# Five ready tiles of attention weights and two exponential slots, in place of four and three, in a two-layer graph kernel

## The chip, the cores and the metric

One core of one Trainium2 chip runs the whole program. The metric is device time in microseconds (us): 262.67 us is the median of three runs of the kernel before, which lie between 262.58 and 264.55. Lower is better.

## The reference

The input is x (2048 nodes, 256 features, float32) and a sparse 0/1 adjacency matrix adj (2048 x 2048). Two graph layers follow each other. Cut to what matters:

```python
h = relu(layernorm(x))
# layer 0: masked attention, a graph convolution, and two sigmoid gates
hd = h @ W_sa
scores = (hd @ a_l)[:, None] + (hd @ a_r)[None, :]
e = where(adj != 0, exp(-leaky_relu(scores, 0.01)), 0.0)
x_a = e / (e.sum(1, keepdims=True) + 1e-05) @ hd
x_b = adj @ (h @ W_gcnb) + b_gcnb
x = x + sigmoid(gate_a * x_a + gate_b * x_b)
# layer 1: attention inside each graph of 64 nodes (ptr), other pairs masked with -1e6
h = relu(layernorm(x))
q, k, v = h @ Wq.T + bq, h @ Wk.T + bk, h @ Wv.T + bv
s = (where(same, q @ k.T / 16, 0) + 2 * adj) * where(same, 1, -1e6)
x = x + (softmax(s) * same) @ v
```

## The kernel before

Five engines run programs written out by hand (one function per engine, under `block.sync`, `block.gpsimd`, `block.scalar`, `block.tensor`, `block.vector`), tied together by semaphores alone. Nothing reorders an engine's program: it issues in the order of the text, and a wait stops all that stands behind it on that engine.

**Layer 0** is a loop over four stages k (columns of 512 nodes each, `CW`), and in a stage over eight pairs q of 128-row tiles. The pair's number over all stages is g = 8k + q. A pair's attention weights (128 x 1024 values) are made in four steps:

- `raw(g)` on ACT (L624, two instructions): the exponential, in float32, into slot g mod `SLOTS` of `e_slot`
- `mask(g)` on DVE (L1462): that slot times the adjacency, in place
- `high(g)` on ACT (L631): the float16 high half of the slot, into place g mod `RING` of `e_hi`
- `low(g)` on DVE (L1468): what the high half left over, into place g mod `RING` of `e_lo`

TensorE (PE) then sums the pair in `attend(k, j)`: for each of its two tiles, 12 matmuls (L972, L974, L976) into the four banks A. Between them it runs `sums(k + 1, ...)`, the graph convolution of the next stage (L948, 16 matmuls a pair). Stage 3 has no such sums.

Three waits bound how far the steps may run ahead. `raw(g)` waits until `low(g - SLOTS)` is done, since it overwrites that slot. `high(g)` waits until PE has attended pair g - `RING`. `attend` waits for `low(g)`.

ACT and DVE run in step with PE by program order: in iteration g of the loop, ACT has `raw(g + RING)` and then `high(g + RING - 1)`, and DVE has `mask(g + RING)` and then `low(g + RING - 1)`. Other work stands between: on DVE `keep_b` (sums into `xb`), `gate_sums`, `add_mix`, `counts` (from L1584 on) and others. At a stage's start (q = 0, k >= 1) DVE first has `denominators(k - 1)` (L1614), which waits until PE has attended the whole stage before; then ACT has `keep_a` (L693, the results out of the banks A) and two tanh. `attend(k, 0)` writes those banks and waits for `keep_a`; in stages 1 and 2 it stands behind 16 `sums`.

Ahead of the loop ("the lead-in"), the first weights are made between the last products of the layer's setup: ACT has `hd_high(g)` (L616, out of PE's banks), `raw(0..3)`, `high(0..2)`, and as its last copy `keep_row(3)` (L608, the row of scores `s_row`). PE's loop starts with `query_key` (L985), and that waits for `keep_row(3)`. DVE has `hd_low`, `mask(0..3)`, `low(0..2)` and the last two `keep_b(0, r)`.

After pair 31 comes **layer 1**, a pipeline over eight pairs p of tiles: PE turns h1 (L1019), ACT and DVE split it into halves (`h1T_high` L723, `h1T_low` L1657), and PE multiplies (`keys`, `values`, L896) and so on. Its first steps stand inside stage 3 already: `turn_h1(0)` in pair 29, `keys(0)` between the two tiles of pair 30. `keys(0)` waits for `h1T_low(0)`, which on DVE stands behind the last `low`, `shifts` and `counts`.

Of the kernel before, what the change touches and what calls it, by code (L numbers as in the profile page):

```python
# [6 lines left out]
F32 = mybir.dt.float32  # L7
# [23 lines left out]
def two_graph_layers(nc, x, adj, adj_t, W_sa, W_saT, a_col, W_gcnb, b_gcnb, gate_w, gate_b, ptr,  # L31
                     Wq, Wk, WvT, bq_bk, bv, out):
    N, D = x.shape
# [3 lines left out]
    KT = D // P  # L37
    CT = 4
    NC = NT // CT
    CW = CT * P  # L40
    RING, SLOTS = 4, 3
    NQ = NT // 2
    PAIRS = NQ * NC
    PW = 2 * CW
# [7 lines left out]
    with ExitStack() as ctx:  # L52
        def sb(name, shape, dt=F32):
            return ctx.enter_context(nc.sbuf_tensor(name, shape, dt))
# [9 lines left out]
        e_slot = sb("e_slot", [P, SLOTS * PW])  # L64
        e_hi = sb("e_hi", [P, RING * PW], F16)
        e_lo = sb("e_lo", [P, RING * PW], F16)
# [113 lines left out]
        w_sa = e_slot[:, 0:KT * D].rearrange("p (k d) -> p k d", k=KT)  # L180
        w_b = e_slot[:, 512:512 + KT * WB].rearrange("p (k d) -> p k d", k=KT)
        w_cols = w_b[:, :, D:WB]
        cols_sq = e_slot[:, 2064:2064 + KT * 6].rearrange("p (k c) -> p k c", k=KT)
        w_saT = e_slot[:, 1040:1040 + KT * D].rearrange("p (k d) -> p k d", k=KT)
        junk_a = e_hi[:, :].bitcast(F32)[:, 0:3 * KT * D].rearrange("p (w k d) -> p w k d", w=3, k=KT)
        at_least = e_lo[:, 0:NT * NP].bitcast(BF16).rearrange("p (t c) -> p t c", c=NP)
# [25 lines left out]
        score_row = adjt[:, 2 * NT * D + N:2 * NT * D + 2 * N]  # L212
        c_all = adjt[:, 3 * NT * D:3 * NT * D + NT]
        mask_row = s_row
        fac_row = e_hi[:, :].bitcast(F32)
        prob_row = e_lo[:, :].bitcast(F32)
        probT_row = e_slot


# [163 lines left out]
        def wait(eng, signal, value):  # L383
            if value > 0:
                eng.wait_ge(signal, value)
# [9 lines left out]
        def adjt_words(k, j, first, count):  # L395
            at = (k % 2) * CHUNK + j * CW + first
            return adjt[:, at:at + count]

        def slot_words(g):
            return e_slot[:, (g % SLOTS) * PW:(g % SLOTS + 1) * PW]  # L400

        def high_words(g):
            return e_hi[:, (g % RING) * PW:(g % RING + 1) * PW]

        def low_words(g):
            return e_lo[:, (g % RING) * PW:(g % RING + 1) * PW]
# [176 lines left out]
        def _(eng):  # L583
# [22 lines left out]
            def keep_row(c):  # L606
                eng.wait_ge(rows_summed, c + 1)
                eng.activation(s_row[:, c * CW:(c + 1) * CW], L[:, (c + 1) % 2, :], ACT.Copy) \  # L608
                   .then_inc(rows_kept, 1)
# [9 lines left out]
            def raw(g):  # L619
                k = g // NQ  # L620
                wait(eng, lo_ready, g - SLOTS + 1)
                for n in range(2):
                    j = 2 * (g % NQ) + n
                    ins = eng.activation(slot_words(g)[:, n * CW:(n + 1) * CW], s_row[:, k * CW:(k + 1) * CW],  # L624
                                         ACT.Exp, scale=SLOPE - 1.0, bias=nbias[:, j:j + 1])
                ins.then_inc(raw_ready, 1)

            def high(g):
                eng.wait_ge(mask_ready, g + 1)
                wait(eng, slot_free, g - RING + 1)  # L630
                eng.activation(high_words(g), slot_words(g), ACT.Copy, scale=E_SCALE).then_inc(hi_ready, 1)  # L631
# [50 lines left out]
            hd_high(7)  # L682
            raw(3)
            high(2)
            keep_row(3)
            eng.wait_ge(rows_kept, NC)
            eng.activation(es[:, :], hc[:, :, 2], ACT.Exp, scale=SLOPE, bias=rm[:, 3:4]).then_inc(es_made, 1)
# [588 lines left out]
        def _(eng):  # L1276
# [174 lines left out]
            def keep_b(k, r):  # L1451
                eng.wait_ge(b_summed, CT * k + r + 1)
                eng.tensor_copy(tails[:, r, :], B[:, r % 2, D:D + TAIL]).then_inc(tail_kept, 1)
                eng.scalar_tensor_tensor(out=xb[:, k % 2, r, :], in0=B[:, r % 2, 0:D], scalar=norm_h[:, 0:1],  # L1454
                                         in1=bg_row[:, :], op0=ALU.mult, op1=ALU.add).then_inc(b_kept, 1)

            def mask(g):
                k, q = divmod(g, NQ)
                if q % 2 == 0:
                    eng.wait_ge(adjt_loaded[q // 2], 16 * (k + 1))  # L1460
                eng.wait_ge(raw_ready, g + 1)
                eng.scalar_tensor_tensor(out=slot_words(g), in0=slot_words(g), scalar=1.0,  # L1462
                                         in1=adjt_words(k, 2 * q, 0, PW), op0=ALU.min, op1=ALU.mult) \
                   .then_inc(mask_ready, 1)

            def low(g):
                eng.wait_ge(hi_ready, g + 1)
                eng.scalar_tensor_tensor(out=low_words(g), in0=slot_words(g), scalar=E_SCALE,  # L1468
                                         in1=high_words(g), op0=ALU.mult, op1=ALU.subtract) \
                   .then_inc(lo_ready, 1)  # L1470
# [19 lines left out]
            hd_low(7)  # L1490
            mask(3)
            low(2)
            keep_b(0, 2)
            keep_b(0, 3)
            eng.wait_ge(layer1_loaded, 16 * 5)
            for kk in range(KT):
# [382 lines left out]
```

## Time and profile before

| what | value |
|---|---|
| median of three runs | 262.67 us |
| the profiled execution | 260.9 us, its span 259.1 us |
| PE busy | 227.5 us, 88% of the span |
| DVE busy | 191.8 us, 74% |
| ACT busy | 158.5 us, 61% |
| granted TensorE clock, mean | 0.991 of full |
| chain that ended last | PE 69%, DVE 15%, ACT 8%, issue 4% of the span |
| `attend` (L972, L974, L976) | 768 matmuls of 128 x 257 |
| `sums` (L948) | 512 matmuls |

A row of the timeline gives an instruction's start, its duration, its engine and line, and in brackets how long its engine stood idle before it and what ended that. Two instructions in a row on ACT or DVE start closer together than the duration that stands beside each, because the next starts before the former has landed. The four stages of the loop run from about 59 to about 208 us; layer 1's steps overlap the last of it.

### The profile page before, as it was taken

How to read it: one execution, taken by the hardware profiler on the slowest of the kernel's cores; microseconds unless marked ns; L12 is line 12 of the kernel's file. 1: busy time of each engine (PE TensorE's matmuls, PEld its weight loads, DVE VectorE, ACT ScalarE, POOL GpSimd, SP SyncE). 2: the span in 40 equal slices, each digit the busy share in tenths (PEclk: the TensorE clock that was granted, in tenths of full speed). 3: DMA queues.
4: the chain of work that ended last, by engine and by line, in shares of the span. 5: the costliest groups of instructions: out<-in, count | busy, mean ns of one | idle time of the engine just before them, and what ended most of it. 6: DMA issues, size and time to landing. Idle time of an engine off the chain costs nothing.

```text
span 259.1 us, 5318 instructions
## 1 busy us (share of the span) xinstructions
PE 227.5 (88%) x2032; PEld 192.9 (74%) x2032; DVE 191.8 (74%) x481; ACT 158.5 (61%) x303; POOL 37.9 (15%) x77
## 2 busy tenths in 40 slices
PE   0688999998998999999999999999967849599962
PEld 0557887887886888888888888878855747488851
DVE  3589878699695686699963999936993366787864
ACT  3568727896666683946736937439865343577650
POOL 2442400000020000011000011000220112434440
PEclk9999999999999999999999999999997999999999
DMA  6999296029874000840400000000000000011113
GB/s 177 343 389 334 27 393 250 3 77 343 277 277 166 0 3 6 320 162 5 160 0 4 1 3 0 3 0 3 0 0 3 0 1 3 1 42 43 62 62 127
DMA packets 20091, 26.34 MB, mean 102 GB/s; under 512 B 1888, under 2 KB 11872, under 8 KB 20064
## 3 DMA queue, kind: packets, MB, share of 16 engines
q1 hardware_dynamic: 19520, 25.72, 28.9%
q8 instruction: 17, 0.28, 0.4%
q10 hardware_dynamic: 544, 0.27, 0.4%
q14 instruction: 10, 0.08, 0.1%
HBM read 23.88 MB, written 2.10 MB: 100 GB/s over the span
## 4 chain that ended last, share of the span: by engine, by line
PE 69%; DVE 15%; ACT 8%; issue 4%; DMA 2%; SPq 1%; DVEq 0%; ACTq 0%
PE bank_b L948 20%; PE bank_a L972 9%; PE bank_a L974 9%; PE bank_a L976 8%; PE bank_a L896 7%; PE bank_l L896 4%; PE bank_b L896 3%; DVE e_lo L1468 2%; DMA e_slot<-in_W_saT 2%; PE bank_a L1087 2%; PE bank_l L888 1%; DVE st6b L1641 1%; ACT adjt L591 1%; PE bank_a L1065 1%; DVE x_all L1636 1%
## 5 line engine op out<-in xcount | busy, mean ns | idle before, releaser
L972 PE MATMUL bank_a<-hd,e_hi 128*128 128x257 f16 x256 | 70.3, 275 | 1.5 <-DVE e_lo L1468 0.9
L974 PE MATMUL bank_a<-hd,e_hi 128*128 128x257 f16 x256 | 70.7, 276 | 0.0
L976 PE MATMUL bank_a<-hd,e_lo 128*128 128x257 f16 x256 | 69.9, 273 | 0.0
L948 PE MATMUL bank_b<-hb,adjt 128*128 128x259 f16 (+1 forms) x512 | 66.7, 273 | 0.2 <-DVE xb L1454 0.2
L948 PEld LDWEIGHTS bank_b<-hb,adjt 128*128 128x128 bf16 x512 | 49.4, 97 | 7.3 <-DVE xb L1454 0.5
L631 ACT ACTIVATE e_hi<-e_slot 128x1024 f16<-128x1024 f32 x32 | 33.7, 1052 | 33.8 <-PE bank_a L976 19.9
L1462 DVE SCALAR_TENSOR_TENSOR e_slot<-e_slot,adjt 128x1024 f32<-128x1024 f32 x32 | 39.0, 1219 | 8.6 <-ACT e_slot L624 8.6
L1468 DVE SCALAR_TENSOR_TENSOR e_lo<-e_slot,e_hi 128x1024 f16<-128x1024 f32 x32 | 39.0, 1220 | 8.5 <-ACT e_hi L631 8.5
L624 ACT ACTIVATE e_slot<-s_row,nbias 128x512 f32<-128x512 f32 x64 | 42.3, 710 | 0.3
L972 PEld LDWEIGHTS bank_a<-hd,e_hi 128*128 128x128 f16 x256 | 25.0, 98 | 6.4 <-DVE e_lo L1468 1.3
L976 PEld LDWEIGHTS bank_a<-hd,e_lo 128*128 128x128 f16 x256 | 25.4, 99 | 3.5
L974 PEld LDWEIGHTS bank_a<-hd,e_hi 128*128 128x128 f16 x256 | 24.9, 97 | 3.5
L542 POOL TENSOR_TENSOR rs_all<-veb,half_neg 128x2 f32<-128x2 f32 x8 | 7.3, 917 | 110.9 <-DVE veb L1646 110.9
L896 PE MATMUL bank_l<-adjt,w_qk 128*128 128x256 f16 x96 | 12.5, 282 | 7.0 <-DVE adjt L1657 7.0
L896 PEld LDWEIGHTS bank_l<-adjt,w_qk 128*128 128x128 f16 x96 | 9.1, 100 | 9.6 <-DVE adjt L1657 5.3
L1664 DVE SCALAR_TENSOR_TENSOR adjt<-bank_l,u_s,adjt 128x256 f16<-128x256 f32 x16 | 7.0, 480 | 11.7 <-ACT adjt L730 11.7
L693 ACT ACTIVATE xa<-bank_a,ga 128x256 f32<-128x256 f32 x16 | 6.3, 474 | 14.2 <-DVE ga L1621 14.2
L547 POOL TENSOR_TENSOR adjt<-adjt 128x512 f16<-128x512 f32 x8 | 9.3, 1156 | 32.5 <-ACT adjt L736 32.5
L896 PE MATMUL bank_a<-wb,x_all 128*128 128x262 f16 x96 | 12.9, 287 | 0.7 <-issue 0.6
L896 PE MATMUL bank_b<-w_v,adjt 128*128 128x257 f16 x96 | 12.7, 273 | 0.0
L896 PE MATMUL bank_a<-wsa,x_all 128*128 128x256 f16 x96 | 11.8, 272 | 0.4 <-DVE hd L1447 0.4
L896 PEld LDWEIGHTS bank_a<-wb,x_all 128*128 128x128 f16 x96 | 9.6, 102 | 3.1 <-issue 1.0
(216 smaller groups left out, 347.9 us busy)
## 6 DMA issues: line engine op xcount, KB each, us to landing
adjt<-in_adj_t SPq DMA_DIRECT2D x16, 1024.0 KB, 7.9
x_all<-in_x SPq DMA_DIRECT2D x4, 512.0 KB, 5.4
out<-adjt SPq DMA_DIRECT2D x16, 128.0 KB, 1.8
adjt<-in_x SPq DMA_DIRECT2D x3, 512.0 KB, 8.1
diag<-in_adj SPq DMA_DIRECT2D x16, 64.0 KB, 3.5
adjt<-in_x SPq DMA_DIRECT2D x2, 256.0 KB, 3.7
e_slot<-in_L_gnn_W_gcnb ACTq DMA_DIRECT2D x1, 256.0 KB, 3.9
e_slot<-in_W_saT SPq DMA_DIRECT2D x1, 256.0 KB, 5.1
```

The source lines that it names most:

```text
L542: eng.tensor_tensor(rs_all[:, first:last], veb[:, r0:r1], half_neg[:, 0:r1 - r0], ALU.pow) \
L547: eng.tensor_tensor(v16[:, p % 4, :, 1, :], v32[:, p % 2, :, :], v16[:, p % 4, :, 0, :], ALU.subtract) \
L624: ins = eng.activation(slot_words(g)[:, n * CW:(n + 1) * CW], s_row[:, k * CW:(k + 1) * CW], ACT.Exp, scale=SLOPE - 1.0, bias=nbias[:, j:j ...
L631: eng.activation(high_words(g), slot_words(g), ACT.Copy, scale=E_SCALE).then_inc(hi_ready, 1)
L896: mm = eng.matmul(bank, left(kk, a), right(kk, b), start=(kk == 0 and a + b == 0), stop=(kk == KT - 1 and a == 1))
L948: eng.matmul(B[:, r % 2, 0:cols], adjt_block(k, j, r), hb16[:, j, part, 0:cols], start=(j == 0 and part == 0), stop=(j == NT - 1 and part ...
L972: eng.matmul(A[:, r, 0:D + 1], high, hd16[:, j, 0, 0:D + 1], start=(j == 0), stop=False, skip_group_check=True)
L974: eng.matmul(A[:, r, 0:D + 1], high, hd16[:, j, 1, 0:D + 1], start=False, stop=False, skip_group_check=True)
L976: mm = eng.matmul(A[:, r, 0:D + 1], low, hd16[:, j, 0, 0:D + 1], start=False, stop=(j == NT - 1), skip_group_check=True)
L1462: eng.scalar_tensor_tensor(out=slot_words(g), in0=slot_words(g), scalar=1.0, in1=adjt_words(k, 2 * q, 0, PW), op0=ALU.min, op1=ALU.mult) \
L1468: eng.scalar_tensor_tensor(out=low_words(g), in0=slot_words(g), scalar=E_SCALE, in1=high_words(g), op0=ALU.mult, op1=ALU.subtract) \
L1664: eng.scalar_tensor_tensor(out=gT16[:, p % 3, c, 1, :], in0=KEYS[:, c * 2 * P:(c + 1) * 2 * P], scalar=u_s[:, c:c + 1], in1=gT16[:, p % 3, ...
```

## The change

The ring of ready weights has five places in place of four, and `e_slot` two slots in place of three. `e_hi` and `e_lo` grow by 2,048 bytes a partition each, and `e_slot` shrinks by 4,096. Two views into the smaller or larger tiles are cut to fit. Since the loop makes `raw(g + RING)` in iteration g, a fifth pair has to be started ahead of it: `raw(4)`, `high(3)`, `mask(4)` and `low(3)` move from the loop's first iteration into the lead-in, and each later step of the loop stands one pair earlier. By the same formula `raw(g)` now waits for `low(g - 2)`.

```diff
-    RING, SLOTS = 4, 3
+    RING, SLOTS = 5, 2
...
-        cols_sq = e_slot[:, 2064:2064 + KT * 6].rearrange("p (k c) -> p k c", k=KT)
+        cols_sq = e_slot[:, 1552:1552 + KT * 6].rearrange("p (k c) -> p k c", k=KT)
...
-        fac_row = e_hi[:, :].bitcast(F32)
-        prob_row = e_lo[:, :].bitcast(F32)
+        fac_row = e_hi[:, 0:2 * N].bitcast(F32)
+        prob_row = e_lo[:, 0:2 * N].bitcast(F32)
...
             raw(3)
             high(2)
+            raw(4)
+            high(3)
             keep_row(3)
...
             low(2)
+            mask(4)
             keep_b(0, 2)
+            low(3)
             keep_b(0, 3)
```

The lead-in on ACT before, from `hd_high(5)` to the first `raw` of the loop (`hd` is written by `hd_high`, `e_slot` by `raw`, `e_hi` by `high`, `s_row` by `keep_row`):

```order
L616 ACTIVATE hd<-bank_a,dp_g 128x256 [waits hd_summed]
L616 ACTIVATE hd<-bank_a,dp_g 128x256
L624 ACTIVATE e_slot<-s_row,nbias 128x512 x2
L616 ACTIVATE hd<-bank_a,dp_g 128x256 [waits hd_summed]
L616 ACTIVATE hd<-bank_a,dp_g 128x256
L631 ACTIVATE e_hi<-e_slot 128x1024 [waits mask_ready]
...
L624 ACTIVATE e_slot<-s_row,nbias 128x512 [waits lo_ready]
L624 ACTIVATE e_slot<-s_row,nbias 128x512
L631 ACTIVATE e_hi<-e_slot 128x1024 [waits mask_ready]
L608 ACTIVATE s_row<-bank_l 128x512 [waits rows_summed]
L687 ACTIVATE es<-hc,rm 128x16 [waits rows_kept]
```

The same place in the changed kernel:

```order
L624 ACTIVATE e_slot<-s_row,nbias 128x512 [waits lo_ready]
L624 ACTIVATE e_slot<-s_row,nbias 128x512
L616 ACTIVATE hd<-bank_a,dp_g 128x256 [waits hd_summed]
...
L624 ACTIVATE e_slot<-s_row,nbias 128x512 [waits lo_ready]
L624 ACTIVATE e_slot<-s_row,nbias 128x512
L631 ACTIVATE e_hi<-e_slot 128x1024 [waits mask_ready]
L624 ACTIVATE e_slot<-s_row,nbias 128x512 [waits lo_ready]
L624 ACTIVATE e_slot<-s_row,nbias 128x512
L631 ACTIVATE e_hi<-e_slot 128x1024 [waits mask_ready]
L608 ACTIVATE s_row<-bank_l 128x512 [waits rows_summed]
L689 ACTIVATE es<-hc,rm 128x16 [waits rows_kept]
```

`raw(2)` has gained a wait on `lo_ready`, and `raw(4)` and `high(3)` now stand ahead of `keep_row(3)`.

Stage 3 on DVE before, from the `mask` of pair 30 to `counts` (`e_slot` is written by `mask`, `e_lo` by `low`, `x_all` to `veb` by `add_mix`, `nb_all` by `shifts`, `owned` by `counts`):

```order
L1462 SCALAR_TENSOR_TENSOR e_slot<-e_slot,adjt 128x1024 [waits raw_ready,adjt_loaded3]
L1468 SCALAR_TENSOR_TENSOR e_lo<-e_slot,e_hi 128x1024 [waits hi_ready]
L1636 SCALAR_TENSOR_TENSOR x_all<-xa,x_all 128x512 [waits half_ready,th_ready]
...
L1646 TENSOR_SCALAR veb<-mvb 128x2 [waits mvb_ready]
L1462 SCALAR_TENSOR_TENSOR e_slot<-e_slot,adjt 128x1024 [waits raw_ready]
L1468 SCALAR_TENSOR_TENSOR e_lo<-e_slot,e_hi 128x1024 [waits hi_ready]
L1651 SCALAR_TENSOR_TENSOR nb_all<-mvb,rs_all 128x2 [waits rs_ready] x2
L1468 SCALAR_TENSOR_TENSOR e_lo<-e_slot,e_hi 128x1024 [waits hi_ready]
L1584 TENSOR_TENSOR owned<-tails,onehot 128x4x34 x2
```

And in the changed kernel, from the `mask` of pair 31:

```order
L1464 SCALAR_TENSOR_TENSOR e_slot<-e_slot,adjt 128x1024 [waits raw_ready]
L1470 SCALAR_TENSOR_TENSOR e_lo<-e_slot,e_hi 128x1024 [waits hi_ready]
L1640 SCALAR_TENSOR_TENSOR x_all<-xa,x_all 128x512 [waits half_ready,th_ready]
...
L1650 TENSOR_SCALAR veb<-mvb 128x2 [waits mvb_ready]
L1470 SCALAR_TENSOR_TENSOR e_lo<-e_slot,e_hi 128x1024 [waits hi_ready]
L1655 SCALAR_TENSOR_TENSOR nb_all<-mvb,rs_all 128x2 [waits rs_ready] x2
L1588 TENSOR_TENSOR owned<-tails,onehot 128x4x34 x2
```

One `mask` and one `low` fewer stand in stage 3; they have moved through the stages ahead of it into the lead-in.

## Rows read from the trace of the kernel before

**Rows 1.** Waits of PE by what ended them: total us, times, longest us

```profile
PE bank_l L896 <- DVE adjt L1657: 7.0, 3, 3.3
...
PE bank_a L972 <- DVE e_lo L1468: 0.9, 1, 0.9
```

**Rows 2.** Timeline of ACT, lead-in: start us, duration us, instruction, [idle before <-releaser]

```profile
51.74 1.33 ACT L624 ACTIVATE e_slot<-s_row,nbias 128x512 f32<-128x512 f32 x2
53.22 0.84 ACT L616 ACTIVATE hd<-bank_a,dp_g 128x256 f16<-128x256 f32 x2
...
56.15 1.33 ACT L624 ACTIVATE e_slot<-s_row,nbias 128x512 f32<-128x512 f32 x2
57.37 1.05 ACT L631 ACTIVATE e_hi<-e_slot 128x1024 f16<-128x1024 f32 x1
58.32 0.59 ACT L608 ACTIVATE s_row<-bank_l 128x512 f32<-128x512 f32 x1
```

**Rows 3.** Timeline of DVE, lead-in

```profile
51.24 1.22 DVE L1468 SCALAR_TENSOR_TENSOR e_lo<-e_slot,e_hi 128x1024 f16<-128x1024 f32 x1
...
54.51 1.22 DVE L1462 SCALAR_TENSOR_TENSOR e_slot<-e_slot,adjt 128x1024 f32<-128x1024 f32 x1
55.65 1.22 DVE L1468 SCALAR_TENSOR_TENSOR e_lo<-e_slot,e_hi 128x1024 f16<-128x1024 f32 x1
```

**Rows 4.** Timeline of PE, the loop's first instruction

```profile
59.17 1.97 PE L985 MATMUL bank_l<-wqk_in 128*128 128x256 f32 x8 [1.02 <-ACT s_row L608]
```

**Rows 5.** Timeline of DVE, stage 1, from its start to stage 2's

```profile
101.41 0.16 DVE L1614 SCALAR_TENSOR_TENSOR den<-es,bank_a 128x4 f32<-128x4 f32 x1 [0.73 <-issue]
...
106.44 1.22 DVE L1462 SCALAR_TENSOR_TENSOR e_slot<-e_slot,adjt 128x1024 f32<-128x1024 f32 x1 [2.06 <-ACT e_slot L624]
...
110.66 1.22 DVE L1468 SCALAR_TENSOR_TENSOR e_lo<-e_slot,e_hi 128x1024 f16<-128x1024 f32 x1
...
116.04 1.23 DVE L1462 SCALAR_TENSOR_TENSOR e_slot<-e_slot,adjt 128x1024 f32<-128x1024 f32 x1
117.18 1.22 DVE L1468 SCALAR_TENSOR_TENSOR e_lo<-e_slot,e_hi 128x1024 f16<-128x1024 f32 x1
...
120.72 1.21 DVE L1462 SCALAR_TENSOR_TENSOR e_slot<-e_slot,adjt 128x1024 f32<-128x1024 f32 x1
121.86 1.22 DVE L1468 SCALAR_TENSOR_TENSOR e_lo<-e_slot,e_hi 128x1024 f16<-128x1024 f32 x1
...
137.13 0.16 DVE L1614 SCALAR_TENSOR_TENSOR den<-es,bank_a 128x4 f32<-128x4 f32 x1 [2.14 <-PE bank_a L976]
```

**Rows 6.** Timeline of ACT, stage 1

```profile
105.01 1.32 ACT L624 ACTIVATE e_slot<-s_row,nbias 128x512 f32<-128x512 f32 x2
...
123.11 1.34 ACT L624 ACTIVATE e_slot<-s_row,nbias 128x512 f32<-128x512 f32 x2
```

**Rows 7.** Timeline of PE, stage 3's first `attend`, then two of layer 1's `keys`

```profile
174.26 0.27 PE L972 MATMUL bank_a<-hd,e_hi 128*128 128x257 f16 x1 [0.59 <-ACT xa L693]
...
196.00 2.11 PE L896 MATMUL bank_l<-adjt,w_qk 128*128 128x256 f16 x12 [2.76 <-DVE adjt L1657]
...
212.33 1.48 PE L896 MATMUL bank_l<-adjt,w_qk 128*128 128x256 f16 x12 [3.31 <-DVE adjt L1657]
```

**Rows 8.** Timeline of ACT, stage 3, its first `raw`

```profile
176.45 1.32 ACT L624 ACTIVATE e_slot<-s_row,nbias 128x512 f32<-128x512 f32 x2
```

**Rows 9.** Timeline of DVE, stage 3

```profile
183.24 0.69 DVE L1636 SCALAR_TENSOR_TENSOR x_all<-xa,x_all 128x512 f32<-128x512 f32 x1
...
185.18 1.22 DVE L1462 SCALAR_TENSOR_TENSOR e_slot<-e_slot,adjt 128x1024 f32<-128x1024 f32 x1
...
191.74 1.22 DVE L1468 SCALAR_TENSOR_TENSOR e_lo<-e_slot,e_hi 128x1024 f16<-128x1024 f32 x1
...
195.16 0.68 DVE L1657 SCALAR_TENSOR_TENSOR adjt<-bank_l,adjt 128x512 f16<-128x512 f32 x1
```

**Rows 10.** Busy us of each engine in a window, granted clock (PEclk), DMA

```profile
196.00:202.00 6.00, 6.00 (x40) 4.73 (x41) 1.06 (x3) 1.85 (x5) 0.00 (x0) 0.72 0.01 3
```

## The prediction

> **What bounds the kernel now.** I read the page first (PE busy 88% of the span), then PE's waits, then the timelines of ACT, DVE and PE side by side at three places: ahead of the loop, across a whole stage, and in the last stage. The question for each is who waits for whom. PE's table of waits says how much a deeper ring can give: in 32 pairs, `attend` waited for a `low` once, 0.9 us; the larger wait, 7.0 us in three pieces, is layer 1's products waiting for `h1T_low` [rows 1]. The first of those three, 2.76 us, stands inside stage 3, and what ends it is DVE's program order [rows 7, 9]. So in stages 0 to 2 PE sets the pace, and the four steps of a pair hide behind it; DVE sets it at the end of stage 3; and at the loop's start it is ACT: PE's first matmul waits 1.02 us for `keep_row(3)` [rows 4].
>
> **The lead-in, +5.1 us.** Two things change: `raw` waits for the `low` two pairs back, and `raw(4)` and `high(3)` go ahead of `keep_row(3)`. Step by step, in the clock of the trace before:
> - `low(0)` lands at 51.24 + 1.22 = 52.46 [rows 3]. A wait of ACT on a `low` costs 0.03 us more: in stage 1 one landed at 121.86 + 1.22 = 123.08 and the `raw` behind it started at 123.11 [rows 5, 6]. So `raw(2)` starts at 52.49, not 51.74 [rows 2].
> - ACT can issue 1.22 us after a `raw`'s start (56.15 to 57.37) [rows 2], so `hd_high(6)` starts at 53.71, not 53.22, and DVE, which follows it, has `mask(2)` 0.49 us late, at 55.00, `low(1)` 1.14 us later at 56.14, landing at 57.36 [rows 2, 3].
> - `raw(3)` waits for that: 57.39, not 56.15. A `mask` starts 1.43 us after its `raw` did (105.01 to 106.44) [rows 5, 6], and a `low` 1.14 us after its `mask` (116.04 to 117.18) [rows 5]: `mask(3)` at 58.82, `low(2)` at 59.96, landing at 61.18. `high(2)` fits in between.
> - `raw(4)` starts at 61.21, `high(3)` at 62.43 (`mask(3)` is long done), and `keep_row(3)` 0.95 us later (57.37 to 58.32) [rows 2], at 63.38. It was at 58.32: **+5.06 us** on the path.
> PE's loop starts that much later, at about 64.2 in place of 59.17 [rows 4], and stands idle for 1.02 + 5.06 = 6.1 us. Nothing repays it in stage 0, where PE sets the pace. The other moved steps, `mask(4)` and `low(3)` with two `keep_b`, run beside PE's `query_key`, 1.97 us [rows 4], and first `attend`; if that cover were gone, PE's next wait would be for `bq_wide`, less than 1 us. The smaller `e_slot` and the changed views issue nothing: 0.
>
> **Stages 1 and 2, +3.9 us.** With two slots, `raw(g)` stands behind `low(g - 2)`, which stands behind `mask(g - 1)`: the steps of neighbouring pairs form a circle. Its length is 1.43 (`raw` to `mask`) + 1.14 (`mask` to `low`) + 1.22 (`low` lands) + 0.03 = 3.83 us [rows 5, 6]. Other work of DVE behind a `low` is free up to 1.4 us, while `raw` runs; beyond that it stretches the circle. In a stage two pieces are longer: `add_mix` with `counts`, from 110.66 + 1.14 to 116.04, 4.24 us, which makes the next `raw` 4.24 + 1.14 + 1.14 + 1.25 = 7.77 us after the start of the `low` ahead of it, hence 7.77 - 1.25 = 6.52 us between the two `raw`; and `add_mix` with `keep_b`, from 117.18 + 1.14 to 120.72, 2.40 us, hence 4.68 us [rows 5]. One stage is then: `denominators` to first `raw`, 3.60 (101.41 to 105.01); seven steps from `raw` to `raw`, 5 x 3.83 + 6.52 + 4.68 = 30.35; the last `raw` to the end of its turn on DVE, 1.43 + 1.14 + 1.14 = 3.71. Sum 37.66 us. PE's stage is 137.13 - 101.41 = 35.72 us, and DVE had 2.14 us to spare at its end [rows 5]. So DVE reaches the next `denominators` 37.66 - 35.72 = 1.94 us late, in stages 1 and 2 alike; stage 0 keeps in step, having no `add_mix` and a full ring ahead.
> The ring of five doesn't help here: PE never lacks weights, but DVE's program has the `mask` and `low` of five pairs ahead standing in front of `denominators`, and the banks A are free only after it. At the end of stage 1, the 16 `sums` still cover more than half of the 1.94 us. At the end of stage 2 there are no `sums`, and PE already waited 0.59 us for `keep_a` [rows 7]: all of 2 x 1.94 = **3.88 us** comes through.
> Bounds: below, 0, if the circle closes faster than PE's pair (35.72 / 8 = 4.47 us against 3.83, which is so wherever DVE has no extra work); above, 3.88, plus 0.6 if small late starts of ACT add up. I take 3.88, since the two long pieces are in the rows.
> The Trainium skill, "Trainium Kernel Development and Optimization", section Best Practices, tells one to double-buffer so that transfers overlap compute. Taken as a rule for these slots, two would be enough, this term 0 and the sum 3.6 us. The rows speak against it here: even with three slots a `raw` of stage 1 started 0.03 us behind the `low` it waits for [rows 5, 6].
>
> **Stage 3, -1.5 us.** One `mask` and one `low` fewer are left. From the first `raw` (176.45) [rows 8] I walk in the same way: the second at 180.28, the third at 184.11; the third `mask` can't start before `low` at 182.85, + 1.14, + 1.94 for `add_mix` and `gates_out` (183.24 to 185.18) [rows 9] = 185.93; `low` at 187.07; + 1.14 + 1.87 for the other `add_mix` = 190.08, where the last `low` starts. `shifts` takes 0.15, and from the last `low` to `h1T_low` it is 195.16 - 191.74 = 3.42 us [rows 9]: 190.08 + 0.15 + 3.42 = 193.65, in place of 195.16. So `keys(0)` starts **1.5 us** earlier, and the 0.9 us wait of `attend` is gone with it, inside that figure. All of layer 1 hangs on `keys(0)`.
>
> **The clock, +1.7 and -1.7 us.** After the wait of 2.76 us the granted clock was 0.72 on average over 6 us [rows 10], which is half speed (1.2 GHz) for 3.4 of the 6 us: it costs 6.00 x 0.28 = 1.7 us, and the same twelve matmuls took 2.11 us, where they took 1.48 after a wait of 3.31 us behind a well-filled stretch [rows 7]. Two places change. The hole of 6.1 us at the loop's start is twice as long as either, so I expect half speed behind it: +1.7. Ahead of `keys(0)`, PE now has one wait of about 2.4 us behind a full stretch in place of two waits, like the row that kept its clock: -1.7. The idle 4 us at the start of stage 3 may cost the same again, but PE has 2.4 us to spare there. Bounds for the pair together: -1.7 to +1.7; I take 0.
> The Trainium skill, "TensorE: Matmul & The Clock Gate", Part 1, says that the default state is throttled and activity releases it. By that rule the loop's start is slow for certain, as I have it; at the start of stage 3 it would be too, at no cost to the sum.
>
> **Sum:** 5.06 + 3.88 - 1.50 + 0 = +7.4 us on the profiled 260.9, so 268.3. The median shown is 1.8 us above that execution; the same difference on it is **270.1 us**.
>
> **Rivals.**
> - *The clock falls one way only.* Kept at the loop's start: 268.4; lost in both places: 271.8. The two waits with opposite outcomes speak for leaving both open [rows 7]. 13% each.
> - *Two slots are enough.* DVE's extra work hides and stages 1 and 2 cost nothing: 5.1 - 1.5 = +3.6, 266.3. For it: the plain circle, 3.83, is below PE's 4.47. Against: 4.24 us of other work in one turn. 12%.
> - *The last stage wins.* The lead-in's delay stays on ACT and doesn't reach PE, if `keep_row(3)` is not what PE's first matmul waits for, and what is left is the shorter stage 3 with its clock kept: -1.5 - 1.7 = -3.2, 259.5. It decides if lead-in and boundaries cost under 3.2 us together. Against: the 1.02 us wait names `keep_row(3)` [rows 4]. 3%.
> - *Nothing to see.* Ring and slots change only who idles, because `attend` waited 0.9 us in all [rows 1]: 262.7. Against: the lead-in's wait [rows 4]. 5%.
>
> The forecast itself holds 54%. Its neighbours on the clock reach from 268.4 to 271.8; with 1.5 us around them for the bounds above the range is 266.9 to 273.0 and leaves out 20%. About 1% (2.6 us) can be told from no change; of the cases, the last stage's is faster by more (3%), the empty one within it (5%), the rest slower (92%).
>
> **What the profile after would show.** PE's first matmul of the loop waiting about 6 us for `s_row`, near 64 us; `raw` in the lead-in idle for L1470 of DVE; ACT in stages 1 and 2 waiting for `e_lo` where it waited for PE before; the distance of the `den` rows 35.7, then about 37.7 us; PE idle about 4 us ahead of stage 3's first `attend`; from there to `keys(0)` 20.2 us where it was 21.7. I am wrong if the first wait is under 3 us, or if the `den` rows stay 35.7 us apart.

## The result, and the profile after

The changed kernel takes **270.39 us** (median of five runs, 268.74 to 273.34) against 262.58 us; the ratio is 1.0316, 95% interval 1.0265 to 1.0366: slower by 3.2%. 270.1 us was forecast.

The first trace of the changed kernel was of a slow execution (273.34 us, mean granted clock 0.960), so the rows below are of a second one (269.68 us, its span 267.9 us, clock 0.976). From the lead-in on, lines of the changed kernel stand 2 to 4 further down in the file than before. PE's table of waits, with the columns of [rows 1]:

```profile
PE bank_l L898 <- DVE adjt L1661: 7.1, 3, 3.3
PE bank_l L987 <- ACT s_row L608: 6.0, 1, 6.0
...
PE bank_a L974 <- ACT xa L695: 2.3, 2, 2.0
...
PE bank_b L950 <- DVE xb L1456: 1.6, 2, 1.4
```

The wait of `attend` for a `low`, 0.9 us before [rows 1], is gone. Three others grew: 6.0 us for `keep_row(3)`, where it was 1.02 [rows 4], 2.3 us for `keep_a` at the stages' starts, where it was 0.6, and 1.6 us for `keep_b`, where it was 0.2.

The timeline of ACT in the lead-in, to set against [rows 2]:

```profile
52.30 1.34 ACT L624 ACTIVATE e_slot<-s_row,nbias 128x512 f32<-128x512 f32 x2 [0.64 <-DVE e_lo L1470]
...
57.21 1.33 ACT L624 ACTIVATE e_slot<-s_row,nbias 128x512 f32<-128x512 f32 x2 [1.15 <-DVE e_lo L1470]
...
60.97 1.33 ACT L624 ACTIVATE e_slot<-s_row,nbias 128x512 f32<-128x512 f32 x2 [1.48 <-DVE e_lo L1470]
62.21 1.04 ACT L631 ACTIVATE e_hi<-e_slot 128x1024 f16<-128x1024 f32 x1
63.16 0.57 ACT L608 ACTIVATE s_row<-bank_l 128x512 f32<-128x512 f32 x1
```

Each of `raw(2)`, `raw(3)` and `raw(4)` waits for a `low`, and `keep_row(3)` comes at 63.16 in place of 58.32. PE's first matmul of the loop answers to [rows 4]:

```profile
63.99 3.65 PE L987 MATMUL bank_l<-wqk_in 128*128 128x256 f32 x8 [6.03 <-ACT s_row L608]
```

It starts 4.82 us later, and the same eight matmuls take 3.65 us in place of 1.97. Stage 1 on ACT, and its end on DVE, to set against [rows 5, 6]:

```profile
111.51 1.32 ACT L624 ACTIVATE e_slot<-s_row,nbias 128x512 f32<-128x512 f32 x2
115.25 1.34 ACT L624 ACTIVATE e_slot<-s_row,nbias 128x512 f32<-128x512 f32 x2 [1.48 <-DVE e_lo L1470]
119.09 1.33 ACT L624 ACTIVATE e_slot<-s_row,nbias 128x512 f32<-128x512 f32 x2 [1.45 <-DVE e_lo L1470]
125.59 1.33 ACT L624 ACTIVATE e_slot<-s_row,nbias 128x512 f32<-128x512 f32 x2 [4.22 <-DVE e_lo L1470]
130.27 1.34 ACT L624 ACTIVATE e_slot<-s_row,nbias 128x512 f32<-128x512 f32 x2 [1.44 <-DVE e_lo L1470]
```

```profile
144.20 1.22 DVE L1470 SCALAR_TENSOR_TENSOR e_lo<-e_slot,e_hi 128x1024 f16<-128x1024 f32 x1
145.33 0.15 DVE L1618 SCALAR_TENSOR_TENSOR den<-es,bank_a 128x4 f32<-128x4 f32 x1
```

From `raw` to `raw` it is 3.74 and 3.84 us, then 6.50 behind `add_mix` with `counts`, then 4.68: the circle and its two long turns. The `den` row follows its `low` with no idle time, where DVE had 2.14 us to spare [rows 5]. What PE waited for because of it, at the start of stage 2, inside it, and at the start of stage 3, where it was 0.59 us [rows 7]:

```profile
146.74 0.27 PE L974 MATMUL bank_a<-hd,e_hi 128*128 128x257 f16 x1 [0.24 <-ACT xa L695]
...
165.72 1.07 PE L950 MATMUL bank_b<-hb,adjt 128*128 128x259 f16 x8 [1.40 <-DVE xb L1456]
...
184.44 0.27 PE L974 MATMUL bank_a<-hd,e_hi 128*128 128x257 f16 x1 [2.03 <-ACT xa L695]
```

Stage 3 on DVE, to set against [rows 9]:

```profile
183.03 0.15 DVE L1618 SCALAR_TENSOR_TENSOR den<-es,bank_a 128x4 f32<-128x4 f32 x1
...
200.18 1.22 DVE L1470 SCALAR_TENSOR_TENSOR e_lo<-e_slot,e_hi 128x1024 f16<-128x1024 f32 x1
201.31 0.15 DVE L1655 SCALAR_TENSOR_TENSOR nb_all<-mvb,rs_all 128x2 f32<-128x2 f32 x1
202.05 0.16 DVE L1655 SCALAR_TENSOR_TENSOR nb_all<-mvb,rs_all 128x2 f32<-128x2 f32 x1 [0.59 <-POOL rs_all L542]
...
204.42 0.68 DVE L1661 SCALAR_TENSOR_TENSOR adjt<-bank_l,adjt 128x512 f16<-128x512 f32 x1
```

`h1T_low(0)` starts 21.39 us behind the third `den` row; before it was 22.32 (172.84 to 195.16). Of the 1.5 us that I had worked out, 0.6 went into a wait that the row in the middle shows: `shifts` needs POOL's power (L542), which needs `add_mix`, and the `mask` that used to stand between is gone.

So the second trace splits like this, each piece between two such rows of the two kernels. The forecast's two terms for the clock stand in the second and the fifth piece:

| piece | before | changed | difference | forecast |
|---|---|---|---|---|
| start of PE's loop | 59.17 | 63.99 | +4.82 | +5.06 |
| from there to the first `den` row (clock) | 42.24 | 43.93 | +1.69 | +1.7 |
| first to third `den` row | 71.43 | 75.11 | +3.68 | +3.88 |
| third `den` row to `h1T_low(0)` | 22.32 | 21.39 | -0.93 | -1.5 |
| `h1T_low(0)` to the end | 63.94 | 63.48 | -0.46 | -1.7 |
| span | 259.1 | 267.9 | +8.8 | +7.4 |

### The profile page after: what moved, and what is told of

Its sections match the earlier page's. It is cut to its first block, busy times and chain, and to the rows that moved or that the text cites. A ratio compares the mean times of both kernels' runs of the same rounds, so it can differ in the third digit from the quotient of the medians.

```text
span 271.5 us, 5317 instructions
## 1 busy us (share of the span) xinstructions
PE 233.6 (86%) x2032; PEld 196.1 (72%) x2032; DVE 193.0 (71%) x481; ACT 159.1 (59%) x303; POOL 37.0 (14%) x77
## 4 chain that ended last, share of the span: by engine, by line
PE 40%; DVE 35%; ACT 12%; issue 8%; DMA 2%; POOL 1%; SPq 0%; DVEq 0%; ACTq 0%; POOLq 0%
DVE e_lo L1470 10%; DVE e_slot L1464 8%; PE bank_b L950 7%; ACT e_slot L624 6%; PE bank_a L898 6%; PE bank_l L898 4%; PE bank_b L898 3%; PE bank_a L974 3%; PE bank_a L976 3%; PE bank_a L978 3%; DVE st6b L1645 2%; DVE xa L1632 2%; DVE x_all L1640 2%; PE bank_l L890 2%; DMA e_slot<-in_W_saT 2%
## 5 line engine op out<-in xcount | busy, mean ns | idle before, releaser
L542 POOL TENSOR_TENSOR rs_all<-veb,half_neg 128x2 f32<-128x2 f32 x8 | 7.3, 917 | 116.2 <-DVE veb L1650 116.2
L898 PE MATMUL bank_l<-adjt,w_qk 128*128 128x256 f16 x96 | 14.0, 305 | 7.1 <-DVE adjt L1661 7.1
L898 PEld LDWEIGHTS bank_l<-adjt,w_qk 128*128 128x128 f16 x96 | 9.8, 108 | 10.3 <-DVE adjt L1661 5.3
L898 PE MATMUL bank_a<-wb,x_all 128*128 128x262 f16 x96 | 13.8, 299 | 0.6 <-issue 0.6
L898 PE MATMUL bank_b<-w_v,adjt 128*128 128x257 f16 x96 | 13.5, 284 | 0.0
```

The source lines that it names most:

```text
L542: eng.tensor_tensor(rs_all[:, first:last], veb[:, r0:r1], half_neg[:, 0:r1 - r0], ALU.pow) \
L898: mm = eng.matmul(bank, left(kk, a), right(kk, b), start=(kk == 0 and a + b == 0), stop=(kk == KT - 1 and a == 1))
```

## The experiments

Eleven runs on the chip, each compared with runs of the kernel before on the same chip. The times between `den` rows come from the timeline of DVE. They are given first in one table. "Sizes" is the pair (places in the ring, slots), "loop starts" the start of `query_key` in us, and the two distances between `den` rows are the lengths of stages 1 and 2. Starts and distances stand on one trace each, the ratios on several runs.

| kernel | sizes | loop starts | between `den` rows | ratio (95%) |
|---|---|---|---|---|
| before | 4, 3 | 59.17 | 35.72, 35.71 | 1 |
| e0_again | 5, 2 | 63.99 | 37.41, 37.70 | – |
| e1_two_slots | 4, 2 | 60.06 | 37.46, 37.45 | 1.0271 (1.0147 to 1.0395) |
| e2_five_places | 5, 3 | 61.43 | 35.72, 35.71 | 1.0103 (1.0016 to 1.0190) |
| e3_row_first | 5, 2 | 57.68 | 37.44, 37.70 | 1.0158 (1.0058 to 1.0258) |
| e4_filled | 5, 2 | 64.15 | 37.44, 37.71 | 1.0337 (1.0225 to 1.0448) |
| e5_spread | 5, 2 | 63.74 | 35.72, 35.90 | 1.0198 (1.0079 to 1.0317) |
| e10_row_first | 4, 3 | 58.32 | 35.72, 35.71 | 0.9950 (0.9890 to 1.0009) |
| e6_first_halves | 4, 3 | 59.21 | 35.72, 35.71 | 0.9935 (0.9893 to 0.9977) |
| e7_both_43 | 4, 3 | 58.09 | 35.72, 35.72 | 0.9877 (0.9816 to 0.9938) |
| e8_all_53 | 5, 3 | 57.40 | 35.72, 35.71 | 0.9849 (0.9800 to 0.9898) |
| e9_all_52 | 5, 2 | 58.92 | 35.72, 35.90 | 0.9933 (0.9896 to 0.9970) |

**e0_again**, the changed kernel once more.

> The changed kernel unchanged, for a second trace of it. If its extra low clock belongs to the kernel and not to one execution: query_key near 64 us again at half speed (3.5 to 3.8 us), den rows 37.4 and 37.7 us apart, h1T_low(0) 21.4 us behind the fourth den row's predecessor, ratio 1.03. Whether the clock falls at keys(0) and at the third keys may differ.

Four runs took 269.05 to 273.81 us. The traced one, 269.68 us, is the trace shown above. The low clock at the loop's start is there again; at `keys(0)` it isn't (1.47 us for the twelve matmuls, 2.72 in the first trace). So where the clock falls differs between executions of the same kernel.

**e1_two_slots**, the slots alone:

```diff
-    RING, SLOTS = 4, 3
+    RING, SLOTS = 4, 2
...
-        cols_sq = e_slot[:, 2064:2064 + KT * 6].rearrange("p (k c) -> p k c", k=KT)
+        cols_sq = e_slot[:, 1552:1552 + KT * 6].rearrange("p (k c) -> p k c", k=KT)
```

> Two slots with the old ring of four and the old order of steps: the slot part of the change alone. My theory: raw(3) of the lead-in waits for low(1), so keep_row(3) and PE's loop start about 1.3 us late; the den rows of stages 1 and 2 stand 37.5 us apart in place of 35.7, +3.7 us at stage 3's start; stage 3 is 0.8 us longer, since the circle of raw, mask and low holds there too. Together +5.8 us, ratio 1.022. Rival (the boundaries cost nothing, the whole loss is the lead-in and its clock): +1 to +2 us, ratio 1.005 to 1.008, den rows 35.7 us apart.

The stages are 37.46 and 37.45 us long, 3.48 us more together, so nearly all of the loss at the boundaries belongs to the slots. From the third `den` row to `h1T_low(0)` it is 23.06 us, 0.74 more than before, as expected. The loop started only 0.9 us late, but behind a wait of just 2.27 us the clock was low as well, 1.7 us more than I had put down:

```profile
60.06 3.65 PE L985 MATMUL bank_l<-wqk_in 128*128 128x256 f32 x8 [2.27 <-ACT s_row L608]
```

**e2_five_places**, the ring alone. To make room, the tile `wqk_in` lies in `xa`.

```diff
-    RING, SLOTS = 5, 2
+    RING, SLOTS = 5, 3
-        wqk_in = sb("wqk_in", [P, 4, D])
+        wqk_in = xa
```

> The changed kernel with three slots again and five places: the ring part alone (to fit it, the tile wqk_in of layer 1's weights lies in xa, which is first written when they are no longer read; no instruction changes). My theory: raw(3) no longer waits, raw(4) and high(3) still stand ahead of keep_row(3): PE's loop 2.2 us late, with a hole of 3.2 us and half clock behind it, +1.7 us as after the hole of 2.3 us with two slots; den rows 35.7 us apart, nothing at the boundaries; stage 3 1.6 us shorter (2.3 by the walk, less 0.6 for shifts waiting for POOL's power). Together +2.3 us, ratio 1.009. Rival (five ready pairs pay by themselves, the slots were the whole loss): below 0.995.

As expected up to `h1T_low(0)`: loop +2.26 us, clock +1.7, stages 35.72 and 35.71, `h1T_low(0)` 20.65 us behind the third `den` row, 1.67 less than before. From there to the end the trace has 1.13 us more than before, with low clocks at the first and the third `keys`. Five places alone don't pay: the ratio is 1.0103, and in the trace the lead-in and the clock behind it cost 3.9 us.

**e3_row_first**, the lead-in's part undone:

```diff
+            keep_row(3)
             raw(3)
             high(2)
             raw(4)
             high(3)
-            keep_row(3)
...
             low(2)
-            mask(4)
             keep_b(0, 2)
-            low(3)
             keep_b(0, 3)
```

with `mask(4)` and `low(3)` behind the two `bq_wide` instead.

> The changed kernel with keep_row(3) ahead of raw(3) on ACT, and mask(4) and low(3) behind bq_wide on DVE: the lead-in's part undone, two slots and five places kept. My theory: PE's loop starts near 58.3 us with no hole, so 5.3 us of lead-in and 2.2 us of clock go, and about 0.5 us of the kernel before's own 1.0 us wait too; the boundaries stay (+3.7 us), stage 3 stays (-0.9): +2.3 us on the kernel before, ratio 1.009, den rows still 37.5 us apart. Rival (the loss sits in the loop, the lead-in is absorbed later): ratio 1.025 to 1.03. Rival (boundaries cost nothing): 0.995.

PE's loop starts at 57.68 with no wait and at full clock, and the stages stay 37.44 and 37.70 us. The ratio falls by 1.6 points from the changed kernel's, less than the 2.2 I expected. One reason is new waits in stage 0:

```profile
72.76 0.38 PE L1012 MATMUL bank_l<-sq,ones 128*128 128x4 f32 x2 [1.53 <-DVE sq L1520]
...
78.19 0.40 PE L1005 MATMUL bank_l<-ident_b,onehot 128*34 128x128 bf16 x4 [0.58 <-DVE nsq L1529]
```

DVE, late with the extra pair, now holds up `norm_1` and what follows. From the loop's start to the first `den` row it is 45.11 us, 2.9 more than before, with the clock full. The other reason stands behind `h1T_low(0)`: 64.47 us to the end, 1.0 more than in the changed kernel, with half clock at the third `keys` (2.74 us for its twelve matmuls, 1.73 there).

**e4_filled**, the hole filled:

```diff
+            eng.wait_ge(hd_lo_made, NT - 2)
+            for n in range(44):
+                eng.matmul(A[:, 0, 0:D], hb16[:, 0, 0, 0:P], hb16[:, 0, 0, 0:D], start=True, stop=True)
             eng.wait_ge(hd_lo_made, NT)
```

> The changed kernel with 44 more matmuls of 128 x 256 on PE ahead of the loop, into a bank that nobody reads then: they fill the hole of 6 us and change nothing else. My theory: the granted clock stays full at the loop's start, query_key takes 2.0 us in place of 3.8, and the kernel is 2.2 us faster than the changed one: +5.6 us on the kernel before, ratio 1.021. Rival (the low clock there is hidden, or not due to the idle time): ratio 1.03 as the changed kernel.

This expectation failed in its second half. The 44 matmuls leave 1.21 us of the hole, `query_key` was fast, and the kernel no faster (270.25 us):

```profile
64.15 1.97 PE L987 MATMUL bank_l<-wqk_in 128*128 128x256 f32 x8 [1.21 <-ACT s_row L608]
```

The windows of PE (busy us and count of PE, PEld, DVE, ACT, POOL, then granted clock, DMA) show where the gain went:

```profile
66.00:68.00 2.00, 2.00 (x20) 1.75 (x19) 1.52 (x4) 1.77 (x3) 0.00 (x0) 1.00 0.36 98
68.00:70.00 2.00, 2.00 (x21) 1.99 (x19) 1.82 (x3) 0.75 (x2) 0.00 (x0) 1.00 0.79 233
70.00:72.00 2.00, 2.00 (x15) 1.58 (x15) 1.47 (x8) 0.59 (x1) 0.00 (x0) 0.69 1.05 401
72.00:74.00 2.00, 2.00 (x12) 1.40 (x10) 0.49 (x2) 1.25 (x2) 0.00 (x0) 0.50 1.05 398
```

The low clock came 6 us later, behind `bias_products`, twenty matmuls of one column each (from 68.17 to 70.46), and cost the same: 43.89 us from the loop's start to the first `den` row, 43.93 without the filler. There, in the changed kernel, it had fallen inside the hole, while PE stood idle until 63.99, and was full again by 68 us:

```profile
60.00:62.00 2.00, 0.00 (x0) 0.00 (x0) 0.94 (x1) 1.03 (x2) 0.00 (x0) 0.65 0.96 317
62.00:64.00 2.00, 0.01 (x1) 0.04 (x1) 1.59 (x3) 1.97 (x4) 0.00 (x0) 0.50 1.12 350
64.00:66.00 2.00, 2.00 (x5) 1.64 (x6) 2.00 (x6) 0.76 (x3) 0.00 (x0) 0.50 0.86 247
66.00:68.00 2.00, 2.00 (x10) 1.46 (x9) 1.52 (x4) 1.61 (x3) 0.00 (x0) 0.65 0.66 145
68.00:70.00 2.00, 2.00 (x21) 1.79 (x19) 1.66 (x2) 0.91 (x2) 0.00 (x0) 1.00 1.04 403
```

So the hole did bring the low clock at `query_key`, and filling it didn't save the time. Why a second fall follows is open: in the kernel before, the same twenty matmuls (from 63.19 to 65.47) were followed by full clock.

**e5_spread**, DVE's long turns broken up in stages 1 and 2:

```diff
-                        if q == 1:
+                        if q == (1 if k == LAST else 3):
                             add_mix(k - 1, 0, 2)
-                        if q == 2:
+                        if q == (2 if k == LAST else 5):
                             add_mix(k - 1, 2, CT)
-                        if q == 3:
+                        if q == (3 if k == LAST else 7):
                             shifts(before, before + 2)
```

> The changed kernel with DVE's add_mix of stages 1 and 2 in iterations 3 and 5 in place of 1 and 2, and shifts in iteration 7: the same work, no longer in one turn with counts. My theory (the circle of raw, mask and low, stretched by DVE's other work beyond 1.4 us in a turn): turns of 4.7, 3.8, 4.3, 3.8, 4.3 us and so on, a stage of about 35.9 us, so den rows 35.8 to 36.0 us apart in place of 37.6, and 3.3 us saved on the changed kernel: ratio 1.019. Rival (DVE simply has too much work, wherever it stands): den rows stay near 37.6 us, ratio 1.03.

The same work of DVE, with the same two slots, and the stages are 35.72 and 35.90 us: 3.5 of the 3.7 us come from where DVE's other work stands, not from the number of slots by itself.

**e10_row_first**, the kernel before with `keep_row(3)` ahead of `raw(3)`.

> The kernel before with keep_row(3) ahead of raw(3) and nothing else. My theory: PE's first matmul of the loop no longer waits 1.0 us, starts at 57.7 us and the whole kernel is 1.0 us faster, ratio 0.996, unless norm_1 of stage 0 then waits for DVE. Rival (the wait moves on to hd_lo_made or b_kept): 1.000.

The wait for `s_row` is gone, the loop starts at 58.32 and the first `den` row is 0.84 us earlier. The ratio of 0.9950 agrees, but its interval reaches 1.0009.

**e6_first_halves**, the work ahead of `keys(0)` shortened:

```diff
-                        if q == 5:
+                        if q == 6:
+                            h1T_high(0)
                             normalize(2)
                             normalize(3)
-                        if q == 6:
-                            h1T_high(0)
-                            normalize(4)
                         if q == 7:
                             keys_high(0)
+                            normalize(4)
...
-                    if q == (5 if k == LAST else 1):
+                    if q == 1 and k < LAST:
                         counts(k)
...
                         if q == 6:
                             h1T_low(0)
+                            counts(LAST)
```

> The kernel before with counts of stage 3 behind h1T_low(0) on DVE, and on ACT normalize(2) and normalize(3) behind h1T_high(0): the work ahead of keys(0) shortened. My theory: keys(0) starts 2.0 us earlier, its hole of 2.8 us shrinks to 0.8, the low clock behind it (1.7 us) may go too: ratio 0.986 to 0.992. Rival (layer 1's chain is bound elsewhere, by keep_values or the later keys): within 0.2 us of the kernel before, 1.000.

`keys(0)` starts 2.0 us earlier and at full clock, as expected; but in this trace the third `keys` is slow, behind the same wait that had done no harm in the trace before [rows 7]:

```profile
194.00 1.47 PE L895 MATMUL bank_l<-adjt,w_qk 128*128 128x256 f16 x12 [0.73 <-DVE adjt L1656]
...
208.67 2.70 PE L895 MATMUL bank_l<-adjt,w_qk 128*128 128x256 f16 x12 [3.31 <-DVE adjt L1656]
```

**e7_both_43, e8_all_53 and e9_all_52** put the pieces together: the last two edits on the old sizes; all of e3 and e6 on five places and three slots (with `wqk_in` in `xa`); and all of e3, e5 and e6 on the changed kernel's own sizes.

> Ring of four and three slots as in the kernel before, with keep_row(3) ahead of raw(3) and the shortened work ahead of keys(0). My theory: the two gains lie in different places and add: 1.3 us and 1.7 us, ratio 0.988. Rival (a low clock falls elsewhere once PE's small holes are gone and takes one of them back): 0.993.

> Five places and three slots, keep_row(3) ahead of raw(3), mask(4) and low(3) behind bq_wide, the shortened work ahead of keys(0): all that the deeper ring could bring, with its lead-in off the path. My theory: den rows 35.7 us apart; PE's only waits for a low (0.9 us in stage 3) go too, but stage 0 pays 1.5 us in a wait of norm_1 for small_squares as with two slots: ratio 0.986 to 0.992, no better than the same kernel with four places. Rival (depth pays): 0.982 or less.

> The changed kernel (five places, two slots) with every loss taken out that I know of: keep_row(3) first, mask(4) and low(3) late, add_mix spread, the work ahead of keys(0) shortened. My theory: its boundaries cost 0.2 us in place of 3.7, the lead-in 1 us of waits in stage 0, stage 3 ends 1 us earlier: ratio 0.990 to 0.997, so the loss of the change is the order of work around it and not the sizes. Rival (two slots cost something in any order): above 1.003.

The two gains add (0.9877). With the order of work mended around them, the changed kernel's sizes are a little faster than the kernel before (0.9933). That is not the sizes' doing: the two edits that don't need them give 0.9877, so against those the five places and two slots seem to lose about 0.6 points (medians 259.7 and 258.0 us), though the two intervals overlap. The fastest version that was run is e8_all_53, with a median of 257.1 us against 262.1 and a ratio of 0.9849, just under the range that I had given. I had expected it to pay 1.5 us in `norm_1`; with three slots that wait did not come. Whether five places are better than four is open: the intervals overlap. In the traces `keys(0)` starts 19.19 us behind the third `den` row in e8 and 19.94 in e9, against 21.13 with four places (e7) and 23.16 in the kernel before, which speaks for it.

## Why the prediction was right

- **Lead-in, +5.06.** Right in mechanism and size (+4.82). e3 took it away. The ring alone costs 2.26 us (e2) and the slots alone 0.89 (e1); the other 1.67 us needs both, since only with five places and two slots does `raw(4)` stand ahead of `keep_row(3)` and wait for a `low` there (1.48 us). That `mask(4)` and `low(3)` hide behind `query_key` held in the changed kernel, where no wait for them shows. The price without that cover, "less than 1 us", was too low: in e3, which makes them later, PE's new waits are 1.53 and 0.58 us, and stage 0 is 2.9 us longer.
- **Clock, +1.7 at the start and -1.7 at `keys(0)`.** The first came as written: +1.69 us in the second trace, +2.21 in the first. The second came too, in the second trace: from the first `keys` to the second it is 1.65 us less than before. But the clock fell at the third `keys` instead and took 1.2 us back, so 0.46 us is left; in the first trace it fell at both, and the piece to the end is 2.1 us longer than before. The reason that I gave, a shorter wait, isn't what the rows show: the wait was 2.93 us where it was 2.76, and the clock stayed full in e0_again and e4 (2.94 us), while e10 has the kernel before's own wait (2.75 us) and kept it too. The term was drawn from one execution of the kernel before, and a repeat need not have the fall in that place. A low clock at the start of stage 3, which I had thought possible at no cost, did not come in either trace of the changed kernel; in e3 it did (0.50 in 180 to 182 us), and it cost nothing up to `h1T_low(0)`, 21.40 us behind the third `den` row as against 21.39.
- **Boundaries, +3.88.** +3.68, shown by e1 (slots alone: 3.48), e2 (ring alone: nothing) and e5 (same slots, other order: 0.2 us). Two slips in the working change it by 0.1 us at most: the circle's terms add up to 3.82 us and not 3.83, and DVE's free time in a turn is 3.82 - 2 x 1.14 = 1.54 us and not 1.4. That PE would be idle 4 us ahead of stage 3 was wrong: 2.03 us, since 1.40 us of it came earlier, in a `sums` of stage 2 waiting for a late `keep_b`. I had followed `denominators` alone. The distance between `den` rows came out as worked out all the same.
- **Stage 3, -1.5.** -0.93: right in direction, too large. The step that failed is "`shifts` takes 0.15": it left out a round by POOL that `mask` had covered, a wait of 0.59 us. From stage 3's first `attend` to `keys(0)` it is 20.80 us, where 20.2 was forecast.
- **Rivals.** "Two slots are enough" falls for this order of work and holds, nearly, at the boundaries for another (e5: 0.2 us). "The last stage wins" names gains that are there (0.9 to 1.7 us), too small for what the lead-in costs.
- **The sum.** +7.4 stands against +7.8 of the medians and +8.8 of the pair of traces. Two terms were too favourable, 0.6 us in stage 3 and 1.2 us of clock, and lead-in and boundaries were 0.4 us too dear: that is the 1.4 us between the sum and the traces. That 270.1 lies so near the median of 270.39 is in part luck. The median of the kernel before lies 1.7 us above its traced execution and that of the changed kernel only 0.7 us above its own, which gives back 1.0 us. The upper end of the range should also read 273.3 (271.8 + 1.5) and not 273.0.

## What to carry to other kernels

Where a buffer passes round through three steps on two engines, add up the circle, and then add to each turn what else stands in the program between two of its steps: a buffer count is enough or not for the longest turn, not for the mean one. A deeper ring has to be filled, and the filling stands in the program ahead of something; look what that is before the depth is weighed. When an instruction is moved away from between two others, see what it covered.

## What the runs showed of the hardware

In every trace but e8's the granted clock fell to half at least once after 60 us, and where it fell moved with edits far away and from one execution to the next: behind a wait of 2.27 us in e1, but not behind one of 2.93 us at `keys(0)` of e0_again; at `keys(0)` of the kernel before behind 2.76 us, but not in e10 behind 2.75; at the third `keys`, behind 3.31 us, in e6 and not in the kernel before. A fall at the loop's start cost 1.7 us, and 2.2 in the first trace of the changed kernel. What PE had done just before doesn't settle it: behind the twenty single-column matmuls the clock fell in e4, it fell while they ran in e9 (0.84 in 64 to 66 us, 0.50 in 66 to 68), and it stayed full in the kernel before.

This spread is larger than what most edits here change. The 43 executions of the kernel before that ran beside the experiments took 259.0 to 265.3 us, and the time goes largely with the mean granted clock: the three at 0.998 took 259.0 to 259.7 us, the eight at 0.971 took 263.8 to 265.3. A single trace is one draw from that. The mean clock was 0.998 in e8's trace, 0.992 in e7's, 0.991 in the kernel before's and 0.976 in e0_again's. e8's traced execution, 253.55 us, is 2.6 us faster than any other of its six; part of its lead over e7, whose third `keys` took 2.74 us where e8's took 1.48, may be the clock and not its order of work.

The Trainium skill, "TensorE: Matmul & The Clock Gate", Part 1, says that the default state is throttled and that activity releases it. The rows of e0_again agree: half clock (0.50) in 62 to 64 us, while PE stood idle, and 1.00 from 68 us on, after PE had started at 63.99.
